# Thirty finished semaphore waits added on TensorE ahead of the batch loop of a decoder layer

## What is computed

```python
def layer(x, ctx):
    n = x * rsqrt(mean(x * x) + 1e-6) * norm_w                    # L0: cross attention
    q, k, v = heads64(n @ wq0), heads64(ctx @ wk0), heads64(ctx @ wv0)
    x = x + merge(softmax(q @ k.T) @ v) @ wo0
    x = x + mha16(ln1(x), ln1(x), causal=True) @ mp + mp_b        # L1: self attention
    x = x + mha16(ln2(x), ctx, causal=False) @ cp + cp_b          # cross attention
    return x + relu(ln3(x) @ f1 + f1_b) @ f2 + f2_b               # MLP
```

## Time and profile before

| | us |
|---|---|
| median of 3 runs (5609.79 to 5610.47) | 5610.1 |
| profiled execution, its own time | 5610.45 |
| its span | 5608.5 |
| of it: before the loop (setup and unrolled start) | 173.2 |
| the loop, 61 rounds | 5200.5 |
| after the loop | 234.8 |

### The profile page before, as it was taken

The page is one execution under the profiler, slowest core; times in us unless marked ns, Lnnn a source line. Parts: engine busy times, 40 slices in busy tenths (PEclk is TensorE's granted clock), DMA queues, the critical chain, the costliest instruction groups (busy, mean ns, idle before and its releaser), DMA issues.

```text
span 5608.5 us, 148782 instructions
## 1 busy us (share of the span) xinstructions
PE 5139.2 (92%) x49240; PEld 4212.8 (75%) x49240; DVE 3046.2 (54%) x7975; ACT 4133.7 (74%) x17025; POOL 698.4 (12%) x1229
## 2 busy tenths in 40 slices
PE   5899999999999999999999999999999999999996
PEld 4777777777777777777777777777777777777785
DVE  4555555555555555555555555555555555555553
ACT  2777787787777777777877877777777778778784
POOL 0111111111111111111111111111111111111110
PEclk9999999999999999999999999999999999999997
DMA  3112112121121121121121211211211211212111
GB/s 117 57 54 74 44 69 74 41 72 62 52 72 59 54 74 59 54 74 44 69 74 41 72 63 52 72 59 54 74 59 54 74 46 68 74 41 72 63 61 39
DMA packets 102242, 348.70 MB, mean 62 GB/s; under 512 B 8752, under 2 KB 66928, under 8 KB 68080
## 3 DMA queue, kind: packets, MB, share of 16 engines
q0 software_dynamic: 36864, 268.45, 13.0%
q1 hardware_dynamic: 64496, 68.39, 3.8%
HBM read 315.84 MB, written 20.97 MB: 60 GB/s over the span
## 4 chain that ended last, share of the span: by engine, by line
PE 53%; ACT 27%; issue 13%; DVE 6%; DMA 1%; ACTq 0%; DVEq 0%; POOL 0%; PEldq 0%; SPq 0%; PEld 0%; POOLq 0%
ACT ps L597 21%; PE ps L975 8%; PE ps L977 6%; PE ps L976 6%; PE ps L1173 6%; PE ps L1156 4%; PE ps L1064 4%; PE ps L1145 3%; DVE negmax L808 2%; PE ps L1134 2%; PE ps L1107 2%; PE ps L1122 2%; PE ps L1140 2%; PE ps L1180 2%; ACT k0bd L577 2%
## 5 line engine op out<-in xcount | busy, mean ns | idle before, releaser
L597 ACT ACTIVATE ps<-ps,negmax 128x77 f32<-128x77 f32 (+2 forms) x6144 | 2058.1, 365 | 310.0 <-DVE negmax L808 308.4
L597 ACT ACTIVATION_READ_ACCUMULATOR ps<-ps,negmax 128x1 f32 x6144 | 1454.1, 243 | 0.8
L808 DVE TENSOR_REDUCE negmax<-ps 128x4 f32<-128x308 f32 (+2 forms) x1792 | 924.2, 563 | 225.3 <-PE ps L1074 90.7
L803 DVE TENSOR_TENSOR zTl<-ps,zTh 128x256 fp32r<-128x256 f32 x512 | 210.7, 422 | 957.0 <-ACT zTh L577 956.8
L528 POOL TENSOR_TENSOR small<-small 128x1 f32<-128x1 f32 (+1 forms) x448 | 256.5, 573 | 2900.3 <-DVE small L785 2673.7
L577 ACT CAST zTh<-ps 128x256 fp32r<-128x256 f32 x512 | 193.0, 390 | 559.6 <-PE ps L1180 528.0
L975 PE MATMUL ps<-tail_h,coTh 128*128 128x256 f32 x2048 | 594.3, 290 | 3.4 <-DVE coTl L908 2.8
L976 PE MATMUL ps<-tail_l,coTh 128*128 128x256 f32 x2048 | 573.5, 280 | 0.0
L977 PE MATMUL ps<-tail_h,coTl 128*128 128x256 f32 x2048 | 572.2, 279 | 0.0
L671 ACT ACTIVATE probs<-ps 128x512 f32<-128x512 f32 x768 | 398.7, 616 | 130.6 <-PE ps L1145 130.6
L1173 PE MATMUL ps<-probs,v 128*32 128x256 f32 x2048 | 216.6, 496 | 273.7 <-issue 270.7
(11 more groups left out here) (200 smaller groups left out, 12847.9 us busy)
## 6 DMA issues: line engine op xcount, KB each, us to landing
tail_h<-parted_wo POOLq DMA_DIRECT2D x64, 1024.0 KB, 5.2
tail_l<-parted_wo POOLq DMA_DIRECT2D x64, 1024.0 KB, 8.4
tail_h<-parted_f POOLq DMA_DIRECT2D x64, 1024.0 KB, 5.2
tail_l<-parted_f POOLq DMA_DIRECT2D x64, 1024.0 KB, 7.0
xin<-x_dram SPq DMA_DIRECT2D x64, 256.0 KB, 4.3
x<-x_dram SPq DMA_DIRECT2D x64, 256.0 KB, 2.7
out<-xr SPq DMA_DIRECT2D x64, 256.0 KB, 2.2
cin<-ctx_dram SPq DMA_DIRECT2D x64, 77.0 KB
```

The source lines that it names most:

```text
L597: ins = nc.scalar.activation(scores, scores, ACT.Exp, bias=negmax[w][:, t, h:h + 1], accum_out=sums[w][:, t, h:h + 1])
L808: nc.vector.tensor_reduce(dst, bank(s)[:, 0:heads * width].rearrange("p (h k) -> p h k", h=heads), AX_X, ALU.max, negate=True).then_inc(ma ...
```

## The change

Two blank lines and a loop of 30 waits are added in PE's setup, between the last drain and the wait for `consts_ready`. Each waits for a semaphore value (`consts_in` at 16 * 7) that PE has already waited for as the first thing in its program, and that does not fall again. Two waits share one instruction, so that PE's part ahead of the loop gets 15 instructions more in the built program, and everything behind them in PE's stream, the loop's body included, stands 15 instructions later. Nothing else is changed: the round has the same instructions on every engine, in the same order.

```diff
@@ -950,6 +950,10 @@
                     ins.then_inc(bias_products, 1)
 
                 pe.drain().then_inc(w_bias, 1)
+
+
+            for _ in range(30):
+                pe.wait_ge(consts_in, 16 * 7)
             pe.wait_ge(consts_ready, 1)
             for bank_full in full:
                 pe.sem_inc(bank_full, FIRST)
```

## The result

| | before | changed |
|---|---|---|
| median, us | 5609.9 | 5210.9 (5209.6 to 5211.5, 4 runs) |
| span of the profiled execution, us | 5608.5 | 5209.5 |
| ratio of the runs | | 0.929, 95% interval 0.9274 to 0.9306 |
| mean granted clock of PE over the span | 0.956 | 0.991 |

The kernel became 399 us faster; 204 had been forecast, and 5210.9 lies outside the range of 5350 to 5490. The direction was right, the size was not.

What follows compares the result with a forecast made beforehand. The prediction took PE's stream, busy for 92% of the span, as the bound. It summed 60 rounds x 3.4 us = 204 us gained and 0 for the setup, giving 5406 us, range 5350 to 5490.

Steps and rivals of the forecast that it cites:

- the gaps at L1173: PE's idle time ahead of L1173, 270.7 us in 120 waits, two gaps a round, read as instruction fetching after the branch.
- The block's end nine instructions behind the round's start: In PE's text, the branch target lies 9 instructions short of a 256-instruction block's end, so the next block's fetch idles PE.
- The setup's waits for nothing: Fifteen finished waits in PE's setup cost about 1.6 us of sequencer, covered by later waits, so taken as 0.
- Step (2): At the loop's start, the shift removes the second gap, 2.9 us in 60 rounds; the gap at the branch stays.
- the first gap: PE idle 2.24 us between the old round's last weight load and the new one's first; expected to stay.
- Step (4): PE's clock still falls in most rounds but recovers earlier, about 3.4 us low; gain 3.4 us a round, to 81.95.
- rival (b): PE's clock does not fall any more in the loop: 5.1 us a round gained, 5304 us; chance 0.15.
- Rival (c): PE's block boundary does not follow the count, or its text is held otherwise: second gap remains, 5610 us; chance 0.06.
- Rival (a): Low-clock stretch as long as in the first round: only 2.1 to 2.25 us a round gained, 5481 us; chance 0.15.
- Rival (d): Branch's fetch stuck behind the fetch ahead, within 40 instructions of a block's start: about 2.9 us a round, 5784; chance 0.02.
- The first round: The loop's first round, entered by falling into it without the second gap, would stay at 83.1 us.
- The sum and the range: Over the loop, 60 x 3.4 = 204 us gained, nothing for setup: 5406 us, range 5350 to 5490; chance 0.62.

Runs made afterwards that it cites:

- experiment 1: Kernel before with 140 instructions of finished waits in the setup instead of the change's 15: 5404.96 us, ratio 0.9626.
- experiments 1 and 4: The latter: kernel before with 124 setup instructions and 17 instructions of finished waits in each round, 5562.2 us; changed kernel with the same 17, 5228.4 us.

## Why the prediction was wrong, point by point

- **PE's stream is the bound, and the gaps at L1173 are fetches of its text**: right. No other engine took any of the gain back beyond the 0.11 us in front of `proj.1.0`. PE's waits for DVE and ACT in rounds 2 to 60 come to 62.0 us in all, for 61.7 before. That is 1.05 us a round; the prediction read it as a few tenths, which changed nothing in its sum.
- **The block's end nine instructions behind the round's start**: right to the instruction (8 and 9 in the setup are 395 us apart).
- **The setup's waits for nothing**: the loop begins at 173.4 us for 173.2. The 14 instructions of L956 that the trace shows take 1.6 us, as estimated. The fifteenth carries the wait for `consts_ready`: it has line L957 and comes at 69.9, so PE had waited 6 us there:

```profile
L956 PEldq EVENT_SEMAPHORE  x14: 51/51/51, 61.8 to 63.4; - x14
```

- **Step (2), "the first gap stays: the branch still jumps out of what is held"**: this is the step that failed. The prediction did expect one packet a round fewer, eight for nine, as for seven blocks and one ahead. But it took it that the branch fetches whatever the number of blocks. Its one reason against a store that keeps the round was the nine packets of the kernel before, and these tell nothing of a round with one block fewer. Measured: a branch of 0.2 us, no packet in rounds 2 to 60, and PE idle for 1.41 us a round, where it is 3.51 with the first gap alone. That leaves 2.1 us of gap a round out of the forecast.
- **Step (4), the clock**: followed from (2). With the first gap the clock falls in 48 of 60 rounds and comes back sooner, for 0.98 and 81.97 us a round, where 0.97 to 0.98 and 81.95 were written. Without that gap it does not fall, which rival (b) expected with the gap still there; that rival's 2.2 us for the clock is what the busy time gives (79.56 less 77.34). The 3.2 us a round that the forecast lacks are 2.1 us of gap and 1.1 us of busy time (78.46 less 77.34).
- **Rival (c), and the store of 2,048 instructions of the Trainium skill**: the prediction used the rule as a count of instructions, found that 1,676 would fit before as well, saw nine packets a round against it and put the rule at the value of "no change". By the runs, the store was the right thing and the unit was wrong. In blocks, eight touched and one ahead do not fit in eight places, and seven and one do. The row that spoke against the rule as it was read, nine a round, was in truth one more than eight, and should have led to the question of what eight would do.
- **Rival (a)**: did not come. The first round, from which it was taken, stands behind an idle time of 3.36 us, and rounds 2 to 60 of the changed kernel do not. In experiment 1, where its gap stood, it did not come either.
- **Rival (d)**: not here, but its mechanism showed at two of the eight places that were tried (126 and 127 added). It costs less there than was written: half or most of the rounds do not fetch at all, and a round that does costs 5.0 us more than a free one (145.0 us in 29 rounds, with 126), for 3.2 in experiment 1, so 1.8 more and not 2.9. It also reaches less far than the 40 instructions that were written: the branches that are number 15 and 16 of a block (experiments 1 and 4) show nothing of it.
- **The first round**: 83.1 us were expected again. It took 78.5, since it ends in a branch too, and that one was as short as the others.
- **The sum and the range**: 60 x 3.4 = 204 was measured as 206 us in experiment 1 (5611.0 less 5405.0), with the luck told there. The range reached up to (a) but down only part of the way to (b), at 5304, and even that would have missed 5211. A case with both gaps gone was not among the rivals at all.

## What to carry to other kernels

All of this was seen on PE, with one loop of 1,676 to 1,734 instructions. For such a hardware loop, count in blocks and not in instructions what an engine's body touches, from the block of its first instruction to that of its branch, and count again for the changed kernel. The branch's own duration (0.2 us here against 3.7) and the packets of that engine's instruction queue in a round (none against nine) show whether the body stays in the store; where it is one block too many, a shift of a few instructions can free the branch. A gap of PE is dearer than its idle time when the clock falls on it; here a gap made by a fetch and one made by finished waits cost the same.

## What was not expected of the hardware

A round of 1,676 instructions costs 395 us more or less in 61 rounds for one instruction ahead of the loop (5216.5 and 5611.2 us). With the branch in the first or second instruction of an eighth block, rounds with a branch of 0.2 us and of about 5 us follow each other within one execution: with 126 instructions added strictly by turns from the sixth round on, with 127 in 7 of 60. 31 instructions a round that wait for nothing, about 0.1 us each, cost as much as a branch that fetches: 5405.9 and 5405.0 us.
